# Border tiles summed once into a window over two blocks, and GpSimd's gathers held at tiles 6 and 13

## What is computed

```
agg = segment_sum(x[src] + e, dst)            # e: a small network on the edge's attributes
h   = (1 + eps) * x + agg
h   = relu(ln(h @ w1 + b1) * g1 + be1)        # 256 -> 1024
h   = relu(ln(h @ w2 + b2) * g2 + be2)        # 1024 -> 1024
y   = h @ w3 + b3                             # 1024 -> 256
out = layernorm(x + relu(ln(x + y)))
```

## Time and profile before

| | |
|---|---|
| three timed runs, median (lowest, highest) | 1556.49 us (1520.37, 1563.42) |
| the profiled execution: its time | 1535.62 us |
| its span, first to last instruction | 1533.7 us |
| mean granted TensorE clock | 0.874 |
| TensorE busy | 82% of the span |
| VectorE, GpSimd, ScalarE busy | 63%, 54%, 44% |
| the chain that ended last: TensorE / unknown / issue | 49% / 15% / 14% |

### The profile page before, as it was taken

How to read it: one execution, slowest core, us unless ns; L and a number is a source line. 1 busy time by engine, 2 the same in 40 slices (tenths; PEclk the granted TensorE clock), 3 DMA queues, 4 the chain that set the end, 5 groups by cost and what they waited for, 6 DMA issues and landing times.

```text
span 1533.7 us, 21066 instructions
## 1 busy us (share of the span) xinstructions
PE 1254.0 (82%) x5295; PEld 993.8 (65%) x5295; DVE 959.9 (63%) x2787; ACT 678.4 (44%) x1654; POOL 824.7 (54%) x840
## 2 busy tenths in 40 slices
PE   4888878888879978877877878886888788878997
PEld 3666666666667666766655756665667667656776
DVE  4766666776666776766744655554565556546665
ACT  2455555565555664545332423332443334323443
POOL 6656555666556666654654564443555456544530
PEclk9788889998878989889988988888898889979999
DMA  6435445555455444546654564544555556554530
GB/s 194 114 112 154 140 134 154 159 155 157 141 146 145 133 134 129 157 126 184 186 153 127 154 189 129 148 141 121 158 154 160 153 145 178 156 149 136 161 111 16
DMA packets 106088, 222.13 MB, mean 145 GB/s; under 512 B 20003, under 2 KB 57369, under 8 KB 106010
## 3 DMA queue, kind: packets, MB, share of 16 engines
q0 software_dynamic: 53408, 164.16, 38.3%
q1 hardware_dynamic: 52602, 57.11, 12.1%
HBM read 203.96 MB, written 17.23 MB: 144 GB/s over the span
## 4 chain that ended last, share of the span: by engine, by line
PE 49%; another core or an unknown queue 15%; issue 14%; DVE 10%; ACT 10%; DMA 1%; POOL 0%; DVEq 0%; ACTq 0%; POOLq 0%; SPq 0%
PE ps_z L1307 21%; PE ps_e L1040 8%; PE ps_y L1307 4%; PE ps_sum L1045 4%; PE ps_sum L1047 4%; PE ps_s L1262 3%; ACT msg L1579 3%; DVE msg L2071 2%; DVE msg L2077 2%; ACT msg L1582 2%; ACT aF L1804 2%; PE ps_tr L1376 2%; DVE oh L159 1%; PE ps_w L1141 1%
## 5 line engine op out<-in xcount | busy, mean ns | idle before, releaser
L963 POOL DMA_INDIRECT grow<-table_dram,src_all x401 | 386.0, 963 | 379.5 <-PE ps_s L1262 250.1
L908 POOL DMA_INDIRECT raw<-in_x,src_all x399 | 404.5, 1014 | 257.4 <-DVE msg L2077 143.7
L1307 PE MATMUL ps_z<-w_high,a 128*128 128x512 f32 x784 | 292.3, 441 | 77.3 <-issue 60.5
L2071 DVE SCALAR_TENSOR_TENSOR msg<-raw,w_sb,msg 128x256 fp32r<-128x256 f32 x416 | 183.8, 482 | 212.2 <-ACT msg L1582 139.0
L1040 PE MATMUL ps_e<-we,attr 65*128 65x256 f32 x832 | 254.9, 431 | 47.2 <-DVE msg L2077 36.6
L1045 PE MATMUL ps_sum<-msg,oh 128*128 128x512 f32 x464 | 251.9, 543 | 29.7 <-DVE msg L2077 23.0
L1307 PEld LDWEIGHTS ps_z<-w_high,a 128*128 128x128 f32 x784 | 167.1, 214 | 130.6 <-issue 78.6
L1582 ACT ACTIVATE msg<-ps_e 128x512 fp32r<-128x512 f32 (+1 forms) x220 | 124.1, 564 | 254.3 <-remote 158.9
L1040 PEld LDWEIGHTS ps_e<-we,attr 65*128 65x128 f32 x832 | 175.2, 217 | 94.7 <-issue 62.0
L159 DVE TENSOR_SCALAR oh<-lane,rel 128x128 fp32r<-128x128 f32 x915 | 209.4, 291 | 3.6 <-issue 3.4
L1047 PE MATMUL ps_sum<-msg,oh 128*128 128x512 f32 x464 | 203.0, 437 | 6.3 <-issue 6.2
(11 more groups left out here) (182 smaller groups left out, 1577.8 us busy)
## 6 DMA issues: line engine op xcount, KB each, us to landing
attr<-in_attrT SPq DMA_DIRECT2D x50, 192.0 KB
raw<-in_x,src_all POOLq DMA_INDIRECT x416
grow<-table_dram,src_all POOLq DMA_INDIRECT x401
w_raw<-in_m_w SPq DMA_DIRECT2D x48, 128.0 KB
table_dram<-table SPq DMA_DIRECT2D x23, 256.0 KB
attr<-in_attrT SPq DMA_DIRECT2D x24, 160.0 KB
xs<-in_x SPq DMA_DIRECT2D x24, 128.0 KB
xTb<-in_xT SPq DMA_DIRECT2D x24, 128.0 KB
```

The lines of the kernel that those rows point to most:

```text
L908: pool.indirect_dma_start(out=raw[:, j, :], out_offset=None, in_=x, in_offset=bass.IndirectOffsetOnAxis(ap=src_all[:, q * TILES + j:q * TI ...
L963: pool.indirect_dma_start(out=grow[:, j, :].bitcast(F32), out_offset=None, in_=table_dram, in_offset=bass.IndirectOffsetOnAxis(ap=src_all[ ...
L1307: mm = pe.matmul(acc, left[a], right[b], start=False, stop=stop and a == 1, skip_group_check=True)
L2071: dve.scalar_tensor_tensor(msg[:, j, 1, 0:D], raw[:, j, :], w_sb[:, tile_cols(n, j)], msg[:, j, 0, 0:D].bitcast(F32), ALU.mult, ALU.subtract)
```

## The change

For positions from 3 on, a border tile is summed once. Tile 16 of a block and tile 0 of the next go into the right half of `ps_y` (256 columns), with a one-hot over a window of 128 rows: the upper 64 rows of the block and the lower 64 of the next. `take_h` has a third addition, of the window's upper half into h; after it `carry` adds the lower half into `hbx` for the next position; ScalarE clears the window (`open_window`). Step 0 and tile 0 of step 1 are left out. (Position 2 opens the first window and still sums its own tile 0 and the tile before.) The test `bad` now asks that border tiles lie within 64 rows of the border, in three column ranges in place of two; the targets of this input meet it, and the same program is chosen.

GpSimd's gathers of tiles 6 to 16, for positions 3 to 24, now also wait until all sums of the position before are done, and those of tiles 13 to 16 until h of the position before has been transposed.

```diff
 def row_gather(path, p, b, j):
-    if path.row_free(p, j // 2) > 0:
-        pool.wait_ge(sum_done, path.row_free(p, j // 2))
+    free = path.row_free(p, j // 2)
+    if WINDOWS < p < BLOCKS and j >= FEW_AHEAD:          # 6
+        free = max(free, SUMS * p)
+    if free > 0:
+        pool.wait_ge(sum_done, free)
+        pool.nop(nofuse=True)
+    if WINDOWS < p < BLOCKS and j >= MORE_AHEAD:         # 13
+        pool.wait_ge(h_turned, p)
         pool.nop(nofuse=True)
...
+def add_window_tile(j, slot):
+    for half in range(2):
+        mm = pe.matmul(ps_y[:, D:2 * D], oh[:, slot, :], grow[:, j, half * D:(half + 1) * D],
+                       start=False, stop=False, skip_group_check=True)
+    return mm
...
 def near_step(path, p, c):
...
+    if kind == WINDOW and (c, j) == path.first_window(p):
+        pe.wait_ge(window_open, p - WINDOWS + 1)
...
 def take_h(b, steps, loaded, windows=True):
...
-    dve.tensor_tensor(h[:, :], ps_s[:, D:2 * D], h[:, :], ALU.add).then_inc(h_ready, 1)
+    dve.tensor_tensor(h[:, :], ps_s[:, D:2 * D], h[:, :], ALU.add).then_inc(h_summed, 1)
+    dve.wait_ge(h_summed, b - WINDOWS + 1)
+    dve.wait_ge(y_done, b - 1)
+    dve.tensor_tensor(h[HALF:P, :], ps_y[HALF:P, D:2 * D], h[HALF:P, :], ALU.add).then_inc(h_ready, 1)
...
+def carry(b):                                            # VectorE, behind h_low
+    dve.wait_ge(hb_in, 16 * (b + 1))
+    dve.tensor_tensor(hbx[0:HALF, :], ps_y[0:HALF, D:2 * D], hbx[0:HALF, :], ALU.add)
...
+def open_window(p):                                      # ScalarE, behind h_high and finish_std
+    wait(act, carried, p - WINDOWS)
+    act.activation(ps_y[:, D:2 * D], lane[:, 0:D], ACT.Copy, scale=0.0).then_inc(window_open, 1)
...
+def make_window_lanes():                                 # VectorE, once: three small copies into lane
```

More of the change, by code:

```diff
@@ L82, in __init__, with steps_at, tiles, tile_kind @@
         self.ahead = [k for k in range(LAST_PAIRS, NP) if PAIRS[k][0] + PAIRS[k][1] <= TILES - edge]
+    def steps_at(self, p):
+        if not behind_window(p):
+            return sum_steps_at(p)
+        return [c for c in range(1, SUMS) if any(self.tile_kind(p, c, j) for j in self.tiles(c))]
+    def tiles(self, c):
+        _, j0, m = self.steps[c]
+        return range(j0, j0 + m)
+    def tile_kind(self, p, c, j):
+        span = self.steps[c][0]
+        if behind_window(p) and (c == 0 or span == 0 and j < self.edge):
+            return None
+        if has_window(p) and (span == 1 or span == 0 and j >= TILES - self.edge):
+            return WINDOW
+        return LANES
+    def first_and_last(self, p):
+        steps = self.steps_at(p)
+        if isinstance(p, int) and p == 1:
+            steps = self.ahead[0:1] + steps
+        plain = [(c, j) for c in steps for j in self.tiles(c) if self.tile_kind(p, c, j) == LANES]
+        return plain[0], plain[-1]
+    def first_window(self, p):
+        return [(c, j) for c in self.steps_at(p) for j in self.tiles(c) if self.tile_kind(p, c, j) == WINDOW][0]
     def sum_inc(self, p, c):
@@ L89, in sum_inc, with one_hot_inc @@
             return 1 + len(self.ahead)
+        if behind_window(p):
+            return c + 1 if c == self.steps_at(p)[0] else 1
         return sum_inc_at(p, c)
+    def one_hot_inc(self, p, steps):
+        if behind_window(p):
+            return steps[-1] + 1 if steps[0] == self.steps_at(p)[0] else len(steps)
+        return sum(sum_inc_at(p, c) for c in steps)
     def one_hots(self, p, c):
@@ L1282, in near_step @@
                     span, j0, m = path.steps[c]
[L1283 to L1286, removed]
+                    first, last = path.first_and_last(p)
+                    if c == first[0]:
                         wait(pe, h_ready, p)
@@ L1289, in near_step @@
                     for j in range(j0, j0 + m):
+                        kind = path.tile_kind(p, c, j)
+                        if kind is None:
+                            continue
+                        if kind == WINDOW and (c, j) == path.first_window(p):
+                            pe.wait_ge(window_open, p - WINDOWS + 1)
                         pe.wait_ge(got[j], 16 * path.fills(p + span, j))
-                        mm = add_tile(j, path.slot[c] + j - j0, c == first and j == j0,
-                                      c == last and j == j0 + m - 1)
+                        if kind == LANES:
+                            mm = add_tile(j, path.slot[c] + j - j0, (c, j) == first, (c, j) == last)
+                        else:
+                            mm = add_window_tile(j, path.slot[c] + j - j0)
                     if path.sum_inc(p, c) > 0:
@@ L1384, in sums @@
                 def sums(path, p, first, end):
-                    for c in sum_steps_at(p):
+                    for c in path.steps_at(p):
                         if first <= c < end:
@@ L2326, in near_oh @@
                 def near_oh(path, p, group):
-                    steps = [c for c in range(OH_GROUPS[group][0], OH_GROUPS[group][1] + 1) if c in sum_steps_at(p)]
+                    steps = [c for c in range(OH_GROUPS[group][0], OH_GROUPS[group][1] + 1) if c in path.steps_at(p)]
                     if not steps:
@@ L2467, in iteration @@
                         h_low(i)
+                    if exists(i + 1):
+                        carry(i)
                     if exists(i - 2):
```

68 lines of the change are left out of this document (54 added, 14 removed).

## The result

The changed kernel took 1409.68 us (median of 4 runs, 1406.32 to 1418.96) against 1541.41 us of the kernel before beside it: ratio 0.9266, 95% interval 0.9201 to 0.9331. (The ratio is of the fast executions alone; 1541.41 is the median of all four of the kernel before, and its profiled one, 1535.62 us, was not a fast one.) On two other chips it came to 1431.75 us (ratio 0.9333, 0.9191 to 0.9474) and 1443.36 us (0.9444, 0.9366 to 0.9523). By the ratios that is 85 to 112 us faster. The prediction had 50 us and a range down to 1450: right in direction, too small by a factor of about two.

The account below looks back on a forecast made before the run. Prediction: the loop is bound by how long twelve gathers go on behind h's transpose, delaying TensorE's increments. Terms -56 + 10 - 11 + 7.5 = -49.5 us, from 1556.5 to 1507, rounded to 1505 us; range 1450 to 1553.

Parts of the forecast that it names:

- The wait at tile 6: GpSimd's gathers from tile 6 waiting for the preceding position's sums: binds at most by its tail, 0 (0 to +8) us.
- rival D: Held gathers behind h's transpose and the next five run together over layer 1, making its increment late: 1602 us, chance 0.09.
- The long iterations: Second-stage loop: long iterations beside short ones stay; if holding tile 13 ends them, up to 40 us more, 1465.
- The wait at tile 13: GpSimd's burst ends 3.75 us earlier, so h's transposed copy does too, 15 times: -56 us.
- the burst of three: Tiles 13 to 15, gathered behind h's transpose, disturb TensorE by 0.7 us, 15 times: +10 us (0 to +36).
- The matmuls left out: TensorE's sums: 17 tiles in place of 19 per position from 3 on, -11 us (0 to -19).
- the third addition: Between the sums and h's transpose: taken as 0.5 us, all exposed, 15 times: +7.5 us (0 to +11).
- carry and open_window: Small operations on VectorE and ScalarE, hidden in idle time; if carry is not hidden, +9 us.
- Rival B: y_done stays late, so take_h's wait for it delays h's transpose: 1538 us, chance 0.15.
- Rival C: Increments aren't bound to the burst's end, or the shorter burst otherwise gains nothing: 1553 us, chance 0.09.
- The clock: TensorE's clock drops to half on idle stretches; speaks for the shorter hold, against the y_done wait; priced by rows only.
- about 3 us: TensorE increments falling more than this far into a run of back-to-back gathers arrive late, close to the run's end.

Follow-up runs that it names:

- e10: Windows without the added gather waits (as e1), but GpSimd idles between tiles 5 and 6 and between 12 and 13 from position 3 on: 1464.00 us, ratio 0.9636.
- e5: The kernel before with only 64 of the 128 rows gathered in each tile from position 1 on: 1543.88 us, ratio 1.0143.
- e18: The kernel before with the hold at tile 6 only, no windows: 1492.30 us, ratio 0.9740.
- e16: The changed kernel again, on one chip with the holds alone: 1443.36 us, ratio 0.9444.
- e1: The changed kernel without the two added waits of the gathers; windows, carry and third addition stay: 1722.55 us, ratio 1.1377.
- e17: The kernel before with both holds and no windows, timed again: 1428.78 us, ratio 0.9363.
- e6: e1 without the third addition of h and its wait for y_done: 1724.41 us.
- e7: The changed kernel without the third addition of h and its wait for y_done: 1434.96 us, ratio 0.9415.
- e14: The changed kernel, unaltered, timed on another chip as base for other cuts: 1431.75 us, ratio 0.9333.

## Why the prediction was wrong

**What bounds the kernel** was read rightly: gathers issued back to back delay TensorE's increments to the end of the run, and TensorE with them. e10 shows it in the strict sense, since mere pauses remove most of the delay. That the amount of data is not the cause is shown by e5.

**The step that failed** is "*The wait at tile 6.* ... It binds at most by the tail of the wait: 0 (0 to +8)". With the windows it is worth 1624 against 1410 to 1443 us, without them and alone 2.6%, some 40 us (e18). On the chip of e16 to e18 the two holds without windows give 97 us by the ratio; the sum had 46 for them, and most of what is missing is this term. The reading behind it (all sums have ended when the burst of twelve begins) holds for a usual iteration of the kernel before, but it was applied to a kernel in which the windows move step 2's increment from 4.2 to 3.3 us into the burst. I had worked out that shift and used it for y_done alone; the same shift decides whether tile 4 waits, and with it whether 5 and 12 gathers become 17. This was rival D's mechanism, placed behind the transpose and not here. And the wait does bind: in the changed kernel the last sums end inside the middle burst, their increment is late by the prediction's own mechanism, and GpSimd idles 40.6 us before tile 6. The pause before tile 4 in the kernel before came about by accident; hold 6 puts one in its place that does not vanish.

**The long iterations** were left standing in the sum and taken as an option of up to 40 us. They were nearly the same burst of 17, already in the trace of before: the iteration of 43.4 us from 1337.5 has 17 gathers from 1350.21 on with no pause above 0.8 us (the other two have one of 1.4 us in theirs). GpSimd's timeline there, with its first and last:

```profile
1350.21 0.94 POOL L963 DMA_INDIRECT grow<-table_dram,src_all  x1 [5.64 <-PE ps_s L1262]
1351.92 0.94 POOL L963 DMA_INDIRECT grow<-table_dram,src_all  x1 [0.76 <-PE ps_s L1262]
...
1371.50 1.01 POOL L963 DMA_INDIRECT grow<-table_dram,src_all  x1 [0.30 <-issue]
```

I had their length and their clock in the earlier trace rows and did not look at what the gathers did in them. Nor was 23.5 us seen "once", as the prediction says: four iterations of the kernel before take 23.4 to 23.5 us, each behind one of 38 to 48 us. One look would have shown the price of a joined burst, 12 us in that iteration, and that hold 6 forbids it. (In the kernel before each long iteration is followed by one of 23.5 us, so that the pair costs only 4 to 10 us above two usual ones of 31.0; in e1 no short one follows.)

**The wait at tile 13**, -56 + 10 = -46 us, was near in size. Between hold 6 alone and both it is 1492.30 to 1428.78 without windows (64 us on one chip), and 1478.85 to between 1410 and 1443 with them (36 to 69). That is in part luck. The sum took 3.75 us from each of 15 late copies, behind a burst of nine. In the changed kernel the copy hT comes 1.2 us behind the start of the transpose and not 5, from the burst of seven in place of nine, which alone would be 7.7 x 15 = 116 us (an estimate); the wait before aF takes part of it back, and no run tells how much. The 10 us for the burst of three are neither confirmed nor refuted.

**The matmuls left out**, -11 us, with +7.5 for the third addition, is -3.5 in sum; e16 and e17 give +15 us with overlapping intervals. Without the holds the same edit costs some 208 us (e1), which no term had. carry and open_window are hidden, as costed: no wait in the profile names them.

**Rival B** (y_done) was given 15%: e6 and e7 show the wait at no cost that a run can tell. **Rival C**: no, hT's delay went. **Rival D**: it came about with the windows alone, at 1722 us where I had 1602 for it. My price was one late increment of 6.4 us per iteration; in e1 it is 18 us. The middle burst of seven is its small form in the changed kernel, with aF's 58.3 us of wait; in e14, which is the same kernel, tiles 13 to 15 run into the next gathers in six of 20 iterations.

**The clock** followed: 0.95 in the loop after, 0.87 before, 0.79 in e1's iterations (row below). The Trainium skill (TensorE: Matmul & The Clock Gate, section "HAM oscillation — how this bites in real kernels") puts such losses down to idle gaps of the engine. The trace agrees in part: in the iteration from 973.4 the matmuls of `ps_z` start 0.43 us apart behind the idle 1.57 us before 993.66, and 0.23 us apart from 996.77 on. But idle time alone does not tell the clock: that iteration has 2.55 us of it at 0.94, the one from 1052.7 has 4.1 us at 1.00. The late increment comes first, and the clock adds to what it costs.

```profile
1037.50:1078.90 41.40, 26.92 (x122) 21.75 (x121) 18.24 (x53) 11.39 (x29) 16.10 (x17) 0.79 0.39 117
```

## What to carry to other kernels

When a kernel's usual, long and short iterations have the same instructions, compare what a neighbouring engine does in each of them before pricing anything: the long ones may be the experiment already made. An edit that removes work ahead of a queue can close an accidental pause in it, and cost many times what it saves; ask of every stall in the trace what it keeps apart. And where an engine issues indirect gathers back to back, place their pauses by semaphores in front of the increments on which the longest chain depends.

## What the runs showed of the hardware

While GpSimd issues indirect gathers one each 1.25 us without a pause, increments of TensorE that fall well into the run are seen late: by 4 us in a burst of seven, by 8.5 us in one of twelve, by 18 us in one of 17, in each case 1.7 to 3.2 us after the run's end. In long runs TensorE itself is mostly let through one matmul per 0.7 to 2.1 us. A gather of 64 rows does the same as one of 128. Pauses of 2.8 us, in which GpSimd does other small operations, cut the delay (e10).

How far into the run the edge lies is not one figure. The prediction's "about 3 us" fits y_done in the kernel before (late at 3.35, in time at 2.8) and step 2 (late at 4.2 there, in time at 3.3 in e1). But in e10 the transposes of h of four iterations ended 2.7 to 4.7 us into a run of seven and were copied 0.1 us behind, and so were those of position 2 in e14, 4.9 us into a run of ten. From 6.3 us on, 202 of 211 transposes of h in all the profiles were copied 1.3 to 3.9 us after the end of the run.

What the two engines share for this is not shown by any run here; nor is what sets the edge, or whether other kinds of DMA issued by GpSimd would do the same.
